# Output projection and first FFN product as fp32r products of exact high and low parts, in a six-layer local-attention kernel

## The reference

```
x = attn_layer(shift_tokens(x)) + x     # q,k,v = x @ Wqkv (128 -> 3 x 1024); l2norm, rotary;
                                        # windows of 32 that also see the window before; softmax; out @ Wo (1024 -> 128)
x = ffn_layer(shift_tokens(x)) + x      # layer norm; hg = xn @ W1 + b1 (128 -> 2 x 341);
                                        # a * gelu(gate) @ W2 + b2 (341 -> 128)
```

## Time and profile before

| | |
|---|---|
| median of 3 runs | 3637.79 us (3636.72 to 3644.33) |
| profiled execution, its own time | 3636.09 us |
| its span | 3634.3 us |
| TensorE busy | 3397.6 us, 93% |
| VectorE busy | 3109.7 us, 86% |
| ScalarE busy | 2520.1 us, 69% |
| GpSimd busy | 1849.6 us, 51% |
| mean granted TensorE clock | 0.979 |

### The profile page before, as it was taken

One profiled execution on the slowest core, in us unless ns is written; L12 is line 12 of the kernel. 1 busy time (PEld: TensorE's weight loads), 2 busy tenths in 40 slices (PEclk: granted clock), 3 DMA queues, 4 the chain that ended last, 5 costly groups with the idle time before them and its releaser, 6 DMA issues.

```text
span 3634.3 us, 161649 instructions
## 1 busy us (share of the span) xinstructions
PE 3397.6 (93%) x63524; PEld 2729.1 (75%) x63524; DVE 3109.7 (86%) x6016; ACT 2520.1 (69%) x4543; POOL 1849.6 (51%) x1604
## 2 busy tenths in 40 slices
PE   5857999999999999999999999999999999999997
PEld 2325888878788877788887788887788887788885
DVE  8987888888788888788888788888788888888884
ACT  2015777777777777777777677777677777777774
POOL 1434655554555555456555465555455564555561
PEclk9988999999999999999999999999999999999998
DMA  2002423323333323333233432332423332323333
GB/s 83 12 26 54 103 60 79 75 57 82 87 77 77 71 62 77 89 79 74 57 79 70 96 75 60 76 78 56 107 63 73 79 73 61 77 66 70 79 75 79
DMA packets 186363, 261.00 MB, mean 72 GB/s; under 512 B 31670, under 2 KB 89908, under 8 KB 185396
## 3 DMA queue, kind: packets, MB, share of 16 engines
q1 hardware_dynamic: 186164, 258.24, 31.6%
HBM read 22.30 MB, written 4.19 MB: 7 GB/s over the span
## 4 chain that ended last, share of the span: by engine, by line
PE 83%; issue 8%; DVE 5%; ACT 1%; POOL 1%; SPq 1%; DMA 0%; DVEq 0%; ACTq 0%; POOLq 0%
PE bank L667 10%; PE bank L654 9%; PE bank L719 9%; PE obank L701 8%; PE bank L752 7%; PE bank L630 7%; PE bank L632 5%; PE bank L631 5%; PE bank L677 5%; PE bank L711 4%; PE bank L645 3%; PE bank L759 3%; PE bank L647 2%; PE bank L646 2%; PE bank L739 1%
## 5 line engine op out<-in xcount | busy, mean ns | idle before, releaser
L977 POOL TENSOR_TENSOR qn<-qn,rinv 128x512 f32<-128x512 f32 x768 | 799.0, 1056 | 1305.0 <-DVE rinv L1224 1305.0
L971 POOL TENSOR_TENSOR qn<-ropec,ropes 128x512 f32<-128x512 f32 x768 | 991.3, 1302 | 257.6 <-DVE ropes L1176 216.1
L852 ACT ACTIVATE sq<-bank 128x512 f32<-128x512 f32 x768 | 458.3, 598 | 195.9 <-PE bank L632 169.3
L1184 DVE TENSOR_REDUCE ss<-sq 128x8 f32<-128x512 f32 x768 | 496.4, 676 | 84.8 <-ACT sq L852 84.8
L1175 DVE TENSOR_TENSOR ropec<-bank,rots 128x512 f32<-128x512 f32 x768 | 525.0, 684 | 18.5 <-ACT sq L852 12.1
L1176 DVE TENSOR_TENSOR ropes<-bank,rots 128x512 f32<-128x512 f32 x768 | 521.6, 679 | 0.0
L654 PE MATMUL bank<-ident,qn 128*128 128x128 f32 x3072 | 470.9, 276 | 26.1 <-ACT qT L870 18.8
L654 PEld LDWEIGHTS bank<-ident,qn 128*128 128x128 f32 x3072 | 369.3, 142 | 94.9 <-POOL qn L977 26.1
L667 PEld LDWEIGHTS bank<-kT,qT 64*32 64x32 f32 x24576 | 362.9, 107 | 96.5 <-issue 96.1
L667 PE MATMUL bank<-kT,qT 64*32 64x64 f32 x24576 | 422.2, 217 | 12.6 <-issue 6.7
L630 PE MATMUL bank<-wqkv_hi,xs_hi 128*128 128x512 f32 x768 | 365.5, 476 | 66.8 <-issue 42.7
(11 more groups left out here) (138 smaller groups left out, 6239.6 us busy)
## 6 DMA issues: line engine op xcount, KB each, us to landing
V<-Vt SPq DMA_DIRECT2D x576, 260.0 KB, 4.4
V<-Vt SPq DMA_DIRECT2D x192, 130.0 KB, 4.5
V<-Vt SPq DMA_DIRECT2D x192, 65.0 KB, 4.1
xres<-X SPq DMA_DIRECT2D x96, 128.0 KB, 2.1
X<-x SPq DMA_DIRECT2D x96, 128.0 KB, 2.0
wqkv_raw<-L_ffn_Wqkv SPq DMA_DIRECT2D x6, 1536.0 KB
xraw<-X SPq DMA_DIRECT2D x97, 64.0 KB, 2.0
xraw<-X SPq DMA_DIRECT2D x97, 63.8 KB, 1.9
```

The source lines that it names most:

```text
L971: pool.tensor_tensor(qn[:, c, :], ropec[:, c % ROPE_RING, :], ropes[:, c % ROPE_RING, :], ALU.add).then_inc(rope_sum.sem, 1)
L977: pool.tensor_tensor(heads8(qn[:, c, :]), heads8(qn[:, c, :]), rinv[:, 8 * c:8 * c + 8].unsqueeze(2).broadcast_to([P, 8, DH]), ALU.mult).t ...
L1184: dve.tensor_reduce(ss[:, 8 * c:8 * c + 8], heads8(sq[:, c % 2, :]), AX.X, ALU.add).then_inc(ss_done.sem, 1)
```

## The change

The weights `wo` and `w1` are each kept as two fp32r tiles, the rounded high part (written by ScalarE) and the low part (raw minus high, written by GpSimd, new steps `wd.0''` and `wd.1'''`). The same is done to the two inputs. For `OT`, ScalarE copies the transposed quarter from PSUM to a ring of two fp32 tiles as before, copies it once more into `OT_hi` (new step `oh.u''`), and GpSimd subtracts to get `OT_lo` (new step `ol.u''`). For `xn`, ScalarE copies to `xn_hi` and GpSimd makes `xn_lo` (new step `xl.0''`). TensorE does three fp32r products (high by high, low weight by high, high by low input) for each fp32 product. In `ORDER` the new steps are put in ScalarE's and GpSimd's rows; the rows of TensorE and VectorE are the same.

```
     "act": """
-        xs.0 wa.1 wa.2 tr.0' qk.3'' w1.0''' tr.1' ot.0'' proj.0 proj.1 tr.2' pt.3'' w1.1''' ot.1'' tr.3'
-        mk.0' proj.2 tr.4' proj.3 w1.2''' wc.2''' ot.2'' tr.5' proj.4 tr.6' ot.3'' tr.7' proj.5 proj.6 mk.1'
...
+        xs.0 wa.1 wa.2 tr.0' qk.3'' w1.0''' tr.1' ot.0'' oh.0'' proj.0 proj.1 tr.2' pt.3'' w1.1''' ot.1''
+        oh.1'' tr.3' mk.0' proj.2 tr.4' proj.3 w1.2''' wc.2''' ot.2'' oh.2'' tr.5' proj.4 tr.6' ot.3''
+        oh.3'' tr.7' proj.5 proj.6 mk.1' qk.0' x1.0'' wc.0'' proj.7 mk.2' v.0 mean.0'' qk.1' pt.0' v.1 mk.3'
+        qk.2' v.2 pt.1' v.3 ln.0'' wc.1'' pt.2' wc.3''' """,
...
     "pool": """
-        norm.6' add.0 add.1 add.2 norm.7' add.3 add.4 norm.0 add.5 norm.1 norm.2 add.6 norm.3 norm.4 add.7
-        norm.5 """,
+        ol.0'' norm.6' add.0 add.1 ol.1'' add.2 norm.7' add.3 ol.2'' add.4 ol.3'' norm.0 add.5 norm.1 norm.2
+        add.6 norm.3 norm.4 add.7 norm.5 xl.0'' wd.0'' wd.1''' """,
...
             def c_wo(c, _, layer):
-                pe.wait_ge(w_c, 4 * layer + 1)
-                pe.wait_ge(ot_copied.sem, ot_copied.at(c, 4))
+                pe.wait_ge(w_clo, 2 * layer + 1)
+                pe.wait_ge(ot_lo_done.sem, ot_lo_done.at(c, 4))
                 pe.wait_ge(c_x2.sem, c_x2.at(c - 1, 1))
                 for i in range(8):
-                    mm = pe.matmul(b_c[:, 0:T], wo[:, i, :], OT[:, i, :], start=i == 0, stop=i == 7)
+                    pe.matmul(b_c[:, 0:T], wo_hi[:, i, :], OT_hi[:, i, :], start=i == 0, stop=False)
+                    pe.matmul(b_c[:, 0:T], wo_lo[:, i, :], OT_hi[:, i, :], start=False, stop=False)
+                    mm = pe.matmul(b_c[:, 0:T], wo_hi[:, i, :], OT_lo[:, i, :], start=False, stop=i == 7)
                 mm.then_inc(c_full.sem, 1)
...
             def c_w1(c, j, layer):
                 f0, n = FFB[j]
                 if j == 0:
-                    pe.wait_ge(w_c, 4 * layer + 3)
-                    pe.wait_ge(c_xn.sem, c_xn.at(c, 1))
+                    pe.wait_ge(w_clo, 2 * layer + 2)
+                    pe.wait_ge(xn_lo_done.sem, xn_lo_done.at(c, 1))
...
-                    mm = pe.matmul(b_c[0:n, part * T:(part + 1) * T], w1[:, cols], xn[:], start=True, stop=True)
+                    o = b_c[0:n, part * T:(part + 1) * T]
+                    pe.matmul(o, w1_hi[:, cols], xn_hi[:], start=True, stop=False)
+                    pe.matmul(o, w1_lo[:, cols], xn_hi[:], start=False, stop=False)
+                    mm = pe.matmul(o, w1_hi[:, cols], xn_lo[:], start=False, stop=True)
...
             def b_ot(b, u):
...
+                act.wait_ge(ot_lo_done.sem, ot_lo_done.at(b, u - 1) if u >= 2 else ot_lo_done.at(b - 1, u + 3))
+                act.activation(OT[:, u % 2], b_trB[:].rearrange("p (j q) -> p j q", j=4),
+                               ACT.Copy).then_inc(ot_copied.sem, 1)
+
+            def b_oh(b, u):
+                t, par = UNIT[u]
+                act.wait_ge(ot_copied.sem, ot_copied.at(b, u + 1))
...
+                act.activation(OT_hi[unit], OT[:, u % 2], ACT.Copy).then_inc(ot_hi_done.sem, 1)
...
             def c_ln_(c, n, layer):
...
+                act.activation(xn[:], lnt[:], ACT.Identity, bias=vec[:, 1:2], scale=vec[:, 0:1]).then_inc(c_xn.sem, 1)
                 act.wait_ge(c_full.sem, c_full.at(c - 1, 7))
+                act.wait_ge(c_xn.sem, c_xn.at(c, 1))
+                act.activation(xn_hi[:], xn[:], ACT.Copy).then_inc(xn_hi_done.sem, 1)
...
+            def b_ol(b, u):
+                t, par = UNIT[u]
+                pool.wait_ge(ot_hi_done.sem, ot_hi_done.at(b, u + 1))
+                unit = (slice(0, P), slice(4 * par, 4 * par + 4), slice(t * P, t * P + P))
+                pool.tensor_tensor(OT_lo[unit], OT[:, u % 2], OT_hi[unit].bitcast(F32), ALU.subtract).then_inc(ot_lo_done.sem, 1)
+
+            def c_xl(c, _):
+                pool.wait_ge(xn_hi_done.sem, xn_hi_done.at(c, 1))
+                pool.tensor_tensor(xn_lo[:], xn[:], xn_hi[:].bitcast(F32), ALU.subtract).then_inc(xn_lo_done.sem, 1)
+
+            def w_low(c, layer, k):
+                if k == 0:
+                    pool.wait_ge(w_c, 4 * layer + 1)
+                    pool.tensor_tensor(wo_lo[:], wo_raw[:], wo_hi[:].bitcast(F32), ALU.subtract).then_inc(w_clo, 1)
+                else:
+                    pool.wait_ge(w_c, 4 * layer + 3)
+                    pool.tensor_tensor(w1_lo[:], w1_raw[:], w1_hi[:].bitcast(F32), ALU.subtract).then_inc(w_clo, 1)
...
             pool.wait_ge(x1_saved, 16)
+            for k in range(2):
+                w_low(0, 0, k)
```

More of the change, by code:

```diff
@@ L126, in build @@
         wqkv_lo = sb("wqkv_lo", [P, 3 * INNER], F32R)
-        wo = sb("wo", [P, 8, D])
-        w1 = sb("w1", [P, 2 * FF])
+        wo_hi = sb("wo_hi", [P, 8, D], F32R)
+        wo_lo = sb("wo_lo", [P, 8, D], F32R)
+        w1_hi = sb("w1_hi", [P, 2 * FF], F32R)
+        w1_lo = sb("w1_lo", [P, 2 * FF], F32R)
         w2 = sb("w2", [P, 3, D])
@@ L159, in build @@
         On = sb("On", [P, 2, 512])
-        OT = sb("OT", [P, 8, T])
+        OT = sb("OT", [P, 2, 4, P])
+        OT_hi = sb("OT_hi", [P, 8, T], F32R)
+        OT_lo = sb("OT_lo", [P, 8, T], F32R)
         xres = sb("xres", [P, T])
@@ L168, in build @@
         xn = sb("xn", [P, T])
+        xn_hi = sb("xn_hi", [P, T], F32R)
+        xn_lo = sb("xn_lo", [P, T], F32R)
         gel = sb("gel", [P, 2, T])
@@ L202, in build @@
         const_in = sem("const_in")
+        w_clo = sem("w_clo")
         sim_begun = sem("sim_begun")
@@ L262, in build @@
         ot_copied = per_batch("ot_copied", 4)
+        ot_hi_done = per_batch("ot_hi_done", 4)
+        ot_lo_done = per_batch("ot_lo_done", 4)
+        xn_hi_done = per_batch("xn_hi_done", 1)
+        xn_lo_done = per_batch("xn_lo_done", 1)
         c_full = per_batch("c_full", 8)
@@ L336, in run_slots @@
                     continue
-                if kind == "wc":
+                if kind in ("wc", "wd"):
                     if conv_c is not None and conv_c[0] == lag:
@@ L518, in loads @@
                 hold(sp, sp_held, w_c, 4 * layer)
+                hold(sp, sp_held, w_clo, 2 * layer)
                 load_weights(layer)
@@ L918, in c_ln_ @@
                 act.wait_ge(c_ln.sem, c_ln.at(c, 1))
+                act.wait_ge(xn_lo_done.sem, xn_lo_done.at(c - 1, 1))
+                act.activation(xn[:], lnt[:], ACT.Identity, bias=vec[:, 1:2], scale=vec[:, 0:1]).then_inc(c_xn.sem, 1)
                 act.wait_ge(c_full.sem, c_full.at(c - 1, 7))
-                act.activation(xn[:], lnt[:], ACT.Identity, bias=vec[:, 1:2], scale=vec[:, 0:1]).then_inc(c_xn.sem, 1)
+                act.wait_ge(c_xn.sem, c_xn.at(c, 1))
+                act.activation(xn_hi[:], xn[:], ACT.Copy).then_inc(xn_hi_done.sem, 1)
             steps = {"xs": a_xs, "proj": a_proj, "v": a_v, "tr": a_tr, "mk": b_mk, "qk": b_qk,
-                     "pt": b_pt, "ot": b_ot, "x1": c_x1_, "mean": c_mean, "ln": c_ln_,
+                     "pt": b_pt, "ot": b_ot, "oh": b_oh, "x1": c_x1_, "mean": c_mean, "ln": c_ln_,
                      "w1": c_w1}
@@ L931, in w_cs @@
                     act.wait_ge(c_full.sem, c_full.at(c, 1))
-                    act.activation(wo[:], wo_raw[:], ACT.Copy).then_inc(w_c, 1)
+                    act.activation(wo_hi[:], wo_raw[:], ACT.Copy).then_inc(w_c, 1)
                 elif k == 1:
@@ L937, in w_cs @@
                     act.wait_ge(c_full.sem, c_full.at(c, 7))
-                    act.activation(w1[:], w1_raw[:], ACT.Copy).then_inc(w_c, 1)
+                    act.activation(w1_hi[:], w1_raw[:], ACT.Copy).then_inc(w_c, 1)
                 else:
@@ L979, in a_norm @@
                                    ALU.mult).then_inc(normed.sem, 1)
-            steps = {"add": a_add, "norm": a_norm}
+            def b_ol(b, u):
+                t, par = UNIT[u]
+                pool.wait_ge(ot_hi_done.sem, ot_hi_done.at(b, u + 1))
+                unit = (slice(0, P), slice(4 * par, 4 * par + 4), slice(t * P, t * P + P))
+                pool.tensor_tensor(OT_lo[unit], OT[:, u % 2], OT_hi[unit].bitcast(F32), ALU.subtract).then_inc(ot_lo_done.sem, 1)
[9 more added lines that the diff above has]
+                    pool.tensor_tensor(w1_lo[:], w1_raw[:], w1_hi[:].bitcast(F32), ALU.subtract).then_inc(w_clo, 1)
+            steps = {"add": a_add, "norm": a_norm, "ol": b_ol, "xl": c_xl, "wd": w_low}
             pool.wait_ge(x1_saved, 16)
+            for k in range(2):
+                w_low(0, 0, k)
             pipeline(pool, lambda *z, **k: run_slots(steps, "pool", *z, **k))
@@ L990, in _ @@
             dve.memset(xraw[64:P, 0:1], 0.0)
-            dve.memset(Vt[:], 1.0)
             dve.memset(xsf[64:P, 0:1], 0.0).then_inc(setup, 1)
@@ L1159, in _ @@
             dve.memset(V[64:64 + WIN, 0, 0], 0.0)
+            dve.memset(Vt[:], 1.0)
             dve.memset(ss[:], 1.0).then_inc(setup, 1)
```

8 lines of the change are left out of this document (2 added, 6 removed).

## The result

The changed kernel takes 4665.42 us in the median of four runs (4663.55 to 4673.41), the kernel before 3637.26 beside it. The ratio is 1.283, with a 95% interval of 1.281 to 1.284: 28% slower, 1028 us. The prediction was 4600, with a range of 4380 to 4760. Of the executions of the kernel before that stand beside the experiments, one (beside the last two) took 13561.66 us; it is left out of the ratios.

The account below looks back on a forecast made before the run. TensorE was taken as the bound, busy 33.06 of a 33.38 us slot. Slots of 43.9 us over 94 slots add 987: 3634.3 + 987 - 35 + 10 = 4596, so 4600 us, range 4380 to 4760.

Parts of the forecast that it names:

- The stall: TensorE's `w1.0''` waits for `xl.0''`, queued behind `norm.5` on GpSimd, starting 10.7 us behind `norm.0` and not 2.5.
- the train: GpSimd's gapless six `norm` and three `add` behind `rinv`, in front of `xl.0''`: 9.93 us.
- `xl` and the release: GpSimd's subtraction for `xn_lo`, 0.65 us, and the release of TensorE after it, 0.1: together 0.75 us.
- Rival 3: Faster, if GpSimd's ten operations took 2.5 us or `rinv` came 8 us earlier: 3507 us; chance 2%.
- The loop: The delay closes from `var` through `rinv`, `xl` and `w1.0''` back to `var`, so it can't be worked off ahead.
- The low clock: TensorE, idle about 8 us before `w1.0''`, then runs products 0.43 apart at half speed: 1.6 to 2 us a slot.
- `wo`'s second wait: `wo` waits 1 to 3 us for `OT_lo`, with `ol.2` and `ol.3` around `add.4`; `w1.0''` to `wo` 20.9 us.
- The first rival: Only `xl.0''` stalls, `OT` parts ready in time: 4410 us, or 4260 without the clock loss; chance 20%.
- The products: TensorE's fp32r products start 0.116 us apart; `wo` saves 0.85 and `w1` 0.6, some 1.4 us a slot.
- The second rival: TensorE's products bound by weight loads: 4810 us at 0.19 apart, 5110 with load and product in sequence; chance 8%.
- The sum: A slot of 43.9 us against 33.38, 10.5 longer, over 94 slots: 987 us.
- the layers' ends: Gaps at layer ends partly hide in the stall, less 35 us; the weights' low parts add 10 us.

Follow-up runs that it names:

- the filler: Changed kernel with 16 products of fp32 constants on TensorE in front of its wait for `xn_lo`, queue order kept: 4635.43 us.
- the second kernel: Changed kernel with `ol.2''` moved before `add.3` and `ol.3''` before `add.4` in GpSimd's row, `xl.0''` staying late: 4524.21 us.
- the fifth: Changed kernel with 16 constant products on TensorE before `w1.0''`, plus `ol.2''` before `add.3` and `ol.3''` before `add.4`: 4418.00 us.
- the third kernel: Changed kernel with `xl.0''` behind `add.5`, `wd.1'''` before `norm.0`, `ol.2''` before `add.3` and `ol.3''` before `add.4`: 3838.61 us.

## Why the prediction was right

**The stall.** The step that carried the sum was that `xl.0''` waits for a train of nine. `norm.0` to `w1.0''` was to be 10.7 us and is 10.71 (2309.34 to 2320.05); the train was 9.93 and is 9.85, `xl` and the release 0.75 and are 0.86. Moving the step takes 630 us away, and the split of `w1` alone, with the step behind the train, adds 864. Rival 3, a train in 2.5 us, didn't come.

**The loop.** That the delay can't be worked off showed as forecast: the wait is 8.16 us in one slot and 8.17 in the next.

**The low clock.** The row behind the wait shows the low level as forecast, and the mean granted clock is 0.895 against 0.979. The sign that I gave for it, 0.43 apart, is that of products of 512 columns; those in the stretch have 256 and start 0.21 apart. The size, 1.6 to 2 a slot, was somewhat high: from `w1.0''` to the next slot's first `proj` it is 4.62 us and was 3.11, 1.5 more; the filler is worth 1.27 us up to `wo`, and with the second wait gone 1.4 us a slot in the middle of a layer and 106 us in all. What I missed is that it isn't tied to one wait: take it away at `w1.0''` and it comes at `wo`, in most slots.

**`wo`'s second wait.** `w1.0''` to `wo` was to be 20.9 and is 21.19; the wait is 1.58 (1 to 3 forecast) and goes with the order of `ol`. The first rival, which left it out and gave 4410, falls with that. Its prices were low as well: the second kernel, which has the low clock and no second wait, took 4524 where it gave 4410, and the fifth, which has neither, 4418 where it gave 4260.

**The products.** This is the term that was mis-sized. 0.116 from start to start was near: 0.118. But `wo` takes 3.00 and not 2.8 and a `w1` block 0.8 and not 0.7 (2326.95 to 2327.74 is 0.79, with 0.86 before), because the first product of each group takes 0.20, and in `wo` the last one 0.21 up to the next group (2344.03 to 2344.24). The saving is 0.78 us a slot and not 1.4. It changes the sum by 0.2 in the loop, because only `wo` lies on it in full. The second rival (products bound by their loads, 0.19 or 0.30 apart) is wrong. By the Trainium skill (TensorE: Matmul & The Clock Gate, Part 3, "The mechanism"), a load may run ahead of running products if it goes to the background buffer; the 0.118 agrees with that half of the rule and not with the other, which asks for another row group.

**The sum.** 43.9 us a slot were forecast, and 44.33 is the mean in the middle of a layer: 0.45 times 94, some 42 us of the 65. For the layers' ends the forecast took off 35 in all and put 10 on. Five slots around an end take 236.0 us and took 184.9, 51.1 more, where five slots elsewhere grew by 54.9; over all five ends that takes off 18, and 7 us of the error are there. Four slots of the last layer, of 45.8 to 46.4 us, make another 7, and the rest lies in the first slots. No large errors cancel in the sum.

## What to carry to other kernels

In a pipeline written as one queue for each engine, a new step costs its place and not its length: 0.7 us of GpSimd cost 8 us of TensorE, because nine operations stood in front of it and its consumer fed the chain that starts them. Before adding a step, look up when its input is ready, when its consumer runs, and what stands in its queue between the two; where the engine's free time lies matters and not how much of it there is. And where the engine to be relieved hardly waits, try the relief first with the new work left out: here it was worth 1.4%, less than any way of paying for it.

## What the runs showed of the hardware

fp32r products of 128 x 128 by 256 columns, each with its own load, start 0.118 us apart, and the first of a group costs 0.20. A group of six then takes 0.79 to 0.81 us where four recorded fp32 instructions took 0.86, and one of 24 takes 3.00 where sixteen took 3.65, 18% less.

The fall of the clock isn't a matter of the wait before it alone. Behind a wait of 1.57 to 1.59 us in front of `wo` the products ran 0.12 apart in the changed kernel's slots in the middle of a layer, and fell to 0.21 in four of five in the kernel with the filler. At a layer's end the changed kernel has the fall too (`wo` at 2431.75 takes 4.34 us behind 1.57). With `xl.0''` early it fell in two slots of three, behind 1.91 to 1.93 us each time. In the third kernel, with 0.68 to 0.70 in front of it, `wo` took 3.0 us in each of the 12 slots read, from 2228 to 2663.

The 20 us before the wait's end don't tell the two cases apart either. Here they are in the kernel with `xl.0''` early, first in front of the slot with the fall (`wo` at 2328.51), then in front of the one without (2366.63); TensorE's busy time is the second figure and the granted clock the third from the end:

```profile
2308.00:2328.00 20.00, 17.28 (x285) 14.03 (x283) 15.62 (x29) 16.01 (x30) 20.00 (x18) 1.00 0.49 101
2346.10:2366.10 20.00, 17.49 (x285) 14.05 (x284) 15.62 (x29) 16.06 (x30) 20.00 (x18) 1.00 0.49 100
```

What decides it stays open.

The subtraction on GpSimd takes 1.25 us from start to start for 512 elements and about 0.7 for 256; with fp32 output `add` takes 1.24, so the fp32r output makes no difference that can be seen. In each slot one `add` of the train takes longer, 1.44 us in the changed kernel (2313.57 to 2315.01) in place of 1.27, and VectorE's subtraction of two SBUF tiles, `xs_lo` (2312.87 to 2313.89), runs beside its first 0.3 us; the Trainium skill (SBUF — State Buffer, "SBUF: two separate sides") says that such a VectorE operation and a GpSimd operation share a port. No run here takes that subtraction away.
